# Gated delta rule on one Trainium2 core: the chunk's decay matrix from running sums that are loaded from DRAM, in place of a matrix product

## The chip, the cores and the metric

The kernel runs on one core of one Trainium2 chip, in one launch. The metric is the device time in microseconds. Three runs of the kernel before gave 3124.35, 3131.32 and 3132.2 us, with a median of 3131.32 us.

## The reference

Two layers are computed on x of shape (2, 1024, 256). The first adds a gated delta rule and a routed feed-forward part to x, the second a small chunked linear attention and a sparse feed-forward part. The change touches the first layer's delta rule and the gates that feed it:

```python
beta = jax.nn.sigmoid(b)
g = -jnp.exp(A_log) * jax.nn.softplus(a + dt_bias)
...
def step(S, inp):
    qt, kt, vt, gt, bt = inp
    S = S * jnp.exp(gt)[:, None, None]
    kv = jnp.einsum('hk,hkv->hv', kt, S)
    delta = (vt - kv) * bt[:, None]
    S = S + kt[:, :, None] * delta[:, None, :]
    o = jnp.einsum('hk,hkv->hv', qt, S)
    return (S, o)
```

There are 2 batches, 16 key heads and 32 value heads of width 128, and g is never positive. A chunk of 128 tokens is computed at once. For that each unit (one batch and one value head) needs the matrix exp(G_n - G_p) for tokens n >= p and zero elsewhere, where G is the running sum of g within the chunk. It weighs both the matrix that is solved for the deltas and the one that gives the outputs.

## The kernel before, in words

`front` normalizes and turns the input, `routed_loop` does the routed feed-forward part and, at its end, the gates (`gate_sums` and what follows), `delta_rule` does the delta rule, and `second_layer` the second layer. Only `delta_rule` and the gates in `routed_loop` are touched.

`delta_rule` takes 128 steps, one for each of the 16 key heads (outer) and 8 chunks (inner), and each step holds U = 4 units, 2 batches by 2 value heads. The steps are pipelined by hand over slots: in slot s each engine runs its own `body(s)`, a fixed list of pieces, and each piece works on the step that lies a fixed number of slots back. `S_P = 0` is the projection and the convolution's four taps, `S_S = 1` the SiLU, `S_F = 2` norms, decay matrix, key-query product (`causal` on PE) and scaled values, `S_L = 5` the triangular solve's blocks of 64, `S_D = 6` the state's step, and `S_E = 7` the output projection. Every engine goes through its list in order, and what it waits for is a semaphore in the piece. A loop body holds 16 slots; 16 slots ahead of it and the last 11 behind it are written out.

What PE does in a slot, with the line numbers of the profile: `front_tp` (L622), `state_in` (L522, the state times keys and queries), `x64` (L598), `x16` (L539), `decay` (L633, the running sums' differences as one 128 x 128 by 128 x 512 product), `causal` (L645), `w1` (L555), `w64` (L609), `project(0)` (L680), `solve` (L709), `w2` (L568), `values` (L659), `apply` (L720, L723), `project(1)` (L680), `w3` (L581, L584), `gated_tp` (L734), `zproj` (L697), `project_out` (L749).

The decay matrix goes through four engines. POOL makes `gtri` = mask times g (L377, in `step_gates`), PE multiplies it by a mask (L633), ACT takes the exponential into `ET` (`expo`, L862), and POOL zeroes its lower half (`causal` on POOL, L406). DVE uses `ET` in `strict` (writes `N`, L1121) and `attention` (L1134).

ACT's last pieces in a slot are `evac(1)` (copies `raw` and `conv` out of the second projection's bank, L907 and L908), `squares` (four squares of the gated output with a sum, L895) and `gtev` (copies the turned output into `gT`, L927). `project_out` on PE starts with

```python
                    pe.wait_ge(gT_rdy, t.done())
```

The base blocks of the solve are found on POOL by substitution (`base_first`, `base_rest`) for two steps at a time. `N` goes to DRAM and comes back as `Bk` in another layout, and the results go out and come back as `Tp` and `Wp`. SP issues these transfers and the heads' weights (`weights`), all on one queue and in program order.

## Time and profile before

| | |
|---|---|
| median of three runs | 3131.32 us |
| the profiled execution's own time | 3119.58 us |
| its span, first to last instruction | 3117.6 us |
| mean granted TensorE clock | 0.979 |
| PE busy | 2977.7 us, 96% of the span |
| DVE, ACT, POOL busy | 2341.5, 1771.9, 1693.4 us (75, 57, 54%) |
| steps of `delta_rule` | 128, from 306.8 us (first projection) to about 2786 us (last output projection) |

A timeline row gives the start in us from the span's start, the duration in us, the engine, the line, the operation, what it writes and reads, and in brackets the idle time of the engine ahead of it with what ended it. One row can stand for several instructions (x8). A product in 32-bit floats is recorded as two matmuls. PE is matmul, PEld the weight load ahead of it.

### The profile page before, as it was taken

To read this page: it belongs to the slowest core of one execution; us is meant where nothing else is said; L and a number is where in the kernel's file an instruction comes from. 1 tells how busy PE (TensorE), PEld (TensorE's weight loads), DVE (VectorE), ACT (ScalarE), POOL (GpSimd) and SP (SyncE) were. 2 spreads that over 40 slices of the span, in tenths; PEclk is the share of its full clock that TensorE was granted. 3 is DMA by queue.
4 is the path that set the end of the run, shared out by engine and by line. 5 is a ranking of instruction groups with operands and counts; after the bars stand their busy time and mean duration, and the time that the engine had idled before them with its cause. 6 is when DMAs were issued, how large, how long until landed. Compare 5 with 4: busy or idle time off the path is not lost. (4 is left out here: it accounts for less than half of the span.)

```text
span 3117.6 us, 70222 instructions
## 1 busy us (share of the span) xinstructions
PE 2977.7 (96%) x23017; PEld 2174.3 (70%) x23017; DVE 2341.5 (75%) x4933; ACT 1771.9 (57%) x5794; POOL 1693.4 (54%) x3744
## 2 busy tenths in 40 slices
PE   5998699999999999999999999999999999978998
PEld 4556377777777777777777777777777777764655
DVE  3433588888888888888888888888888888746766
ACT  4322466666666666666666666666666666532332
POOL 2000466676666766676767666766766767610000
PEclk9999799999999999999999999999999999978999
DMA  3000111112112111111111212121111111210000
GB/s 85 1 1 14 27 44 37 44 37 45 42 44 46 40 44 42 44 37 45 37 44 37 47 42 50 39 48 38 44 37 44 37 44 37 46 38 4 7 7 14
DMA packets 447088, 113.77 MB, mean 36 GB/s; under 512 B 350528, under 2 KB 445872, under 8 KB 446704
## 3 DMA queue, kind: packets, MB, share of 16 engines
q1 hardware_dynamic: 446704, 108.99, 15.7%
q8 instruction: 200, 3.28, 0.4%
q14 instruction: 184, 1.51, 0.2%
HBM read 63.85 MB, written 45.09 MB: 35 GB/s over the span
## 5 line engine op out<-in xcount | busy, mean ns | idle before, releaser
L907 ACT ACTIVATE raw<-bank 128x512 f32<-128x512 f32 x256 | 153.3, 599 | 428.8 <-PE bank L680 423.4
L464 POOL TENSOR_TENSOR Tb<-Tb,btmp 64x14 f32<-64x14 f32 (+6 forms) x896 | 327.5, 365 | 70.9 <-POOL btmp L460 1.2
L1175 DVE SCALAR_TENSOR_TENSOR conv<-raw,ckq,conv 128x512 f32<-128x512 f32 x384 | 323.7, 843 | 24.2 <-ACT conv L908 13.2
L460 POOL TENSOR_TENSOR btmp<-Bk,Tb 64x14 f32<-64x14 f32 (+6 forms) x896 | 296.6, 331 | 65.6
L1175 DVE SCALAR_TENSOR_TENSOR conv<-raw,cv,conv 128x512 f32<-128x512 f32 x384 | 292.1, 761 | 13.8 <-ACT conv L908 2.7
L680 PE MATMUL bank<-xnT,wkq 128*128 128x512 f32 x512 | 254.8, 621 | 17.4 <-issue 11.8
L448 POOL TENSOR_SCALAR Tb<-Bk 64x256 f32<-64x256 f32 x64 | 73.7, 1151 | 341.2 <-DMA Bk<-blk_n 341.2
L680 PE MATMUL bank<-xnT,wv 128*128 128x512 f32 x512 | 248.8, 609 | 7.0 <-issue 4.7
L749 PE MATMUL bank<-wout_h,gT 128*128 128x256 f32 x1024 | 249.6, 387 | 1.3 <-ACT gT L927 1.2
L522 PE MATMUL bank<-S,ykq 128*128 128x256 f32 x1024 | 243.2, 379 | 5.8 <-issue 5.8
L852 ACT ACTIVATE sq_kq<-bank 128x128 bf16<-128x128 f32 x512 | 134.9, 278 | 194.6 <-PE bank L622 194.6
L1145 DVE SCALAR_TENSOR_TENSOR S<-S,gs,bank 128x128 f32<-128x128 f32 x512 | 143.7, 343 | 132.4 <-PE bank L720 132.4
L697 PE MATMUL bank<-wz_h,xnT 128*128 128x256 f32 x1024 | 242.4, 380 | 0.0
L406 POOL TENSOR_TENSOR ET<-ET,le 128x512 f32<-128x512 f32 x128 | 179.8, 1405 | 90.9 <-ACT ET L862 90.9
L749 PEld LDWEIGHTS bank<-wout_h,gT 128*128 128x128 f32 x1024 | 186.1, 192 | 43.3 <-ACT gT L927 22.7
L884 ACT ACTIVATE vb<-bank,ty 128x128 f32<-128x128 f32 x512 | 146.5, 369 | 114.2 <-PE bank L659 114.2
L522 PEld LDWEIGHTS bank<-S,ykq 128*128 128x128 f32 x1024 | 184.6, 190 | 26.7 <-issue 7.0
L697 PEld LDWEIGHTS bank<-wz_h,xnT 128*128 128x128 f32 x1024 | 184.6, 190 | 19.9
L709 PEld LDWEIGHTS bank<-R,Wf 128*128 128x128 f32 x1024 | 136.5, 195 | 62.6 <-issue 62.6
L1121 DVE SCALAR_TENSOR_TENSOR N<-ET,ty,bank 128x128 f32<-128x128 f32 x512 | 143.4, 341 | 44.5 <-POOL ET L406 37.6
L895 ACT ACTIVATE sq_gat<-gat 128x128 bf16<-128x128 f32 x512 | 150.7, 304 | 33.1 <-DVE gat L1160 33.1
L939 ACT ACTIVATE gatn<-gat,ty 128x128 f32<-128x128 f32 x512 | 161.9, 390 | 0.1
(350 smaller groups left out, 7543.3 us busy)
## 6 DMA issues: line engine op xcount, KB each, us to landing
blk_n<-N SPq DMA_DIRECT2D x128, 256.0 KB, 2.6
Tp<-blk_t SPq DMA_DIRECT2D x128, 128.0 KB, 2.9
Wp<-blk_w SPq DMA_DIRECT2D x128, 128.0 KB, 3.0
wkq<-in_L_attn_W_qkvz_dram SPq DMA_DIRECT2D x32, 128.0 KB, 2.4
wv<-in_L_attn_W_qkvz_dram SPq DMA_DIRECT2D x16, 256.0 KB, 3.1
Bk<-blk_n SPq DMA_DIRECT2D x64, 64.0 KB, 2.7
blk_t<-Tb SPq DMA_DIRECT2D x64, 64.0 KB, 2.5
blk_w<-Wb SPq DMA_DIRECT2D x64, 64.0 KB, 2.5
```

What stands on the lines that cost most here:

```text
L406: pool.tensor_tensor(ET[:], ET[:], le4[:], ALU.mult).then_inc(ET_rdy, 1)
L460: pool.tensor_tensor(tmp, Bk[:, j, j + 1:].unsqueeze(2).broadcast_to([64, 15 - j, j]), Tb[:, j, 0:j].unsqueeze(1).broadcast_to([64, 15 - j ...
L464: pool.tensor_tensor(Tb[:, j + 1:, 0:j], Tb[:, j + 1:, 0:j], tmp, ALU.subtract).then_inc(row_rdy, 1)
L522: i = pe.matmul(bB[6 + j][:, b], chunk(kq_of(t), t, j, b), S[:, 2 * b:2 * b + 2, :].rearrange("p v n -> p (v n)"), start=True, stop=True)
L680: i = pe.matmul(bank[1 - j][:], w[:, k, j * P:(j + 1) * P], xnT[:, k, q * 512:(q + 1) * 512].rearrange("p (c b n) -> p b c n", c=2, b=B), ...
L697: i = pe.matmul(bB[1][:, b], xnT[:, k, n * P:(n + 1) * P], wz[:, k, :], start=(k == 0), stop=(k == KT - 1))
L749: i = pe.matmul(bB[0][:, h], gT[:, 2 * h + v, :], wout[:, v, :], start=(v == 0), stop=(v == 1))
L884: i = act.activation(vb[t.c % RING][:, u, :], bU[0][:, u], ACT.Copy, scale=ty[t.c][:, VS, u // 2:u // 2 + 1])
L895: i = act.activation(junkg[:, u, :], gat[:, u, :], ACT.Square, accum_out=ty[t.c][:, SSG, u:u + 1])
L907: act.activation(raw[h][:, j, :, 3:], bB[1 - j], ACT.Copy)
L939: i = act.activation(gatn[:, u, :], gat[:, u, :], ACT.Copy, scale=ty[t.c][:, SC, u:u + 1])
L1175: dve.scalar_tensor_tensor(out=conv[h][:, j], in0=raw[h][:, j, :, k:k + 256], scalar=cw[:, j, k:k + 1], in1=conv[h][:, j], op0=ALU.mult, o ...
```

## The change

`gate_sums` already makes the running sums of g within each chunk. `routed_loop` now also copies them (`ab`), keeps them with the other per-token gates (kind `CUM` in the place of `G`), turns them with four transposes, and writes them to DRAM as `decay_rows`, with one row of 128 sums per chunk and unit.

In `delta_rule`, SP loads for each step the four rows onto all 128 partitions (`decays`, 256 KB into one of two tiles `rowb`), a slot before they are used. ACT makes Relu(G_p - row) in place (`clamp`, four instructions, one for each unit) and then exp(-x) into `ET` (`expo`). Both now stand at the end of the slot before the one that uses `ET`. The product on PE, its operand on POOL, and their semaphores are gone. POOL's list is in another order, the copy of the level-64 block into `Wf` goes from DVE (`add_w64`) to ACT (`wev64`), and DVE's six taps of the convolution stand together, alternating between their two halves, with `add_w3` ahead of them.

```diff
-G, BETA, NGAM, GAM, DEC, GLAST = range(NKIND)
+CUM, BETA, NGAM, GAM, DEC, GLAST = range(NKIND)
...
+                def decays(s):
+
+                    t = s.back(S_F - 2)
+                    if not t.live:
+                        return
+                    free = held(sp, t.done(2))
+                    sp.wait_ge(m["made"], 2)
+                    sp.wait_ge(hd["rows_out"], 16)
+                    wait(sp, exp_rdy, free)
+                    sp.dma_start(rowb[t.c % 2][:].rearrange("p (b v) n -> p b (v n)", b=B),
+                                 rows[t.c, :, bass.ds(t.head(), 1), :].rearrange("b h n -> b (h n)").partition_broadcast(P)
+                                 ).then_inc(rowb_in[t.c % 2], 16)
...
                 def body(s):
+                    decays(s)
                     weights(s)
                     base_out(s)
                     dump(s)
...
-                    pool.wait_ge(gs_rdy, t.done())
-                    wait(pool, dt_mm, t.done(1))
-                    pool.tensor_tensor(gtri[:], le4[:], gs[t.c][:, G, :].unsqueeze(2).broadcast_to([P, U, P]),
-                                       ALU.mult).then_inc(gtri_rdy, 1)
...
                 def body(s):
+                    step_gates(s)
+                    causal(s)
                     derive(s)
-                    causal(s)
                     halo(s)
                     base_rest(s)
-                    step_gates(s)
                     base_first(s)
...
-                def decay(s):
-
-                    t = s.back(S_F)
-                    if not t.live:
-                        return
-                    pe.wait_ge(gtri_rdy, t.done())
-                    wait(pe, zz_rdy, t.done(4))
-                    ends(pe, s, araw_rdy, t, -1)
-                    pe.matmul(bank[1][:], m["gt"][:], gtri[:].rearrange("p u n -> p (u n)"), start=True,
-                              stop=True).then_inc(dt_mm, 1)
...
-                        wait(pe, exp_rdy, t.done(2))
+                        wait(pe, zz_rdy, min(t.done(6), STEPS) if t.i is None else t.done(6))
...
+
+                def clamp(s):
+
+                    t = s.back(S_F - 1)
+                    if not t.live:
+                        return
+                    act.wait_ge(rowb_in[t.c % 2], t.pairs(16, 16))
+                    act.wait_ge(gs_rdy, t.done())
+                    for u in range(U):
+                        i = act.activation(rowb[t.c % 2][:, u, :], rowb[t.c % 2][:, u, :], ACT.Relu, scale=-1.0,
+                                           bias=gs[t.c][:, CUM, u:u + 1])
+                    i.then_inc(rel_rdy, 1)
+
                 def expo(s):
-                    t = s.back(S_F)
-                    if not t.live:
-                        return
-                    act.wait_ge(dt_mm, t.done())
+
+                    t = s.back(S_F - 1)
+                    if not t.live:
+                        return
+                    act.wait_ge(rel_rdy, t.done())
                     wait(act, N_rdy, t.done(1))
                     wait(act, attn_rdy, t.done(1))
-                    act.activation(ET[:], bU[1], ACT.Exp).then_inc(exp_rdy, 1)
+                    act.activation(ET[:], rowb[t.c % 2][:], ACT.Exp, scale=-1.0).then_inc(exp_rdy, 1)
 
                 def kdec(s):
...
 
+                def wev64(s):
+
+                    t = s.back(S_L + 1)
+                    if not t.live:
+                        return
+                    act.wait_ge(w64_mm, t.done())
+                    act.activation(Wf[0:64, :, 64:], bG[5][0:64], ACT.Copy).then_inc(w64_rdy, 1)
...
                     xev64(s)
-                    expo(s)
                     normed(s)
+                    wev64(s)
                     evac(s, 0)
                     vscale(s)
                     kdec(s)
                     evac(s, 1)
+                    clamp(s)
                     squares(s)
                     gtev(s)
+                    expo(s)
...
                     dve.tensor_tensor(gat[:].rearrange("p u n -> p (u n)"), gat[:].rearrange("p u n -> p (u n)"),
                                       zz[:].rearrange("p b n -> p (b n)"), ALU.mult).then_inc(gat_rdy, 1)
 
-                def taps(s, j):
+                def taps(s):
 
                     t = s.back(S_P)
                     if not t.live:
                         return
                     h = t.c % 2
                     cw = cv if h else ckq
-                    done = tap_b if j else tap_a
-                    dve.wait_ge(braw_rdy if j else araw_rdy, t.done())
+                    dve.wait_ge(araw_rdy, t.done())
+                    dve.wait_ge(braw_rdy, t.done())
                     for k in (2, 1, 0):
-                        if k < 2:
-                            dve.wait_ge(done[k + 1], t.done())
-                        dve.scalar_tensor_tensor(out=conv[h][:, j], in0=raw[h][:, j, :, k:k + 256],
-                                                 scalar=cw[:, j, k:k + 1], in1=conv[h][:, j], op0=ALU.mult,
-                                                 op1=ALU.add).then_inc(done[k], 1)
+                        for j, done in enumerate((tap_a, tap_b)):
+                            if k < 2:
+                                dve.wait_ge(done[k + 1], t.done())
+                            dve.scalar_tensor_tensor(out=conv[h][:, j], in0=raw[h][:, j, :, k:k + 256],
+                                                     scalar=cw[:, j, k:k + 1], in1=conv[h][:, j], op0=ALU.mult,
+                                                     op1=ALU.add).then_inc(done[k], 1)
...
-                    taps(s, 0)
                     add_w3(s)
-                    taps(s, 1)
+                    taps(s)
                     norm_apply(s)
...
+                def gate_rows():
+
+                    pe.wait_ge(act_rdy, 5)
+                    for q in range(4):
+                        i = pe.transpose(psB[:, 0, q * P:(q + 1) * P], ab[:, q * P:(q + 1) * P], m["ident"][:])
+                    i.then_inc(cum_rdy, 1)
...
                 for j, kind in enumerate((GAM, DEC, GLAST)):
                     for b in range(B):
                         i = act.activation(into(kind, b), of(psH[:, j, :], b), ACT.Exp)
                 i.then_inc(act_rdy, 1)
+
+                act.wait_ge(cum_rdy, 2)
+                act.activation(turned, psB[:, 0, :], ACT.Copy).then_inc(turned_rdy, 1)
+
+            @block.sync
+            def _(sp):
+                sp.wait_ge(turned_rdy, 1)
+                sp.dma_start(rows.rearrange("(q c) b h (v n) -> (c b h v) q n", q=4, v=2),
+                             turned.rearrange("p (q n) -> p q n", q=4)).then_inc(hd["rows_out"], 16)
 
             @block.vector
             def _(v):
...
-                        v.tensor_copy(into(G, b), of(ga[:], b))
                         v.tensor_copy(into(BETA, b), of(gf, b))
 
                 def gate_end():
 
                     v.wait_ge(act_rdy, 5)
+                    for b in range(B):
+                        v.tensor_copy(into(CUM, b), of(ab[:], b))
+                    v.wait_ge(act_rdy, 6)
```

Three places in program order. First ACT in a steady slot, from the second projection's copies to the next slot's squares of keys and queries (`sq_kq`). Before:

```order
L907 ACTIVATE raw<-bank 128x2x256
L908 ACTIVATE conv<-bank,ckq 128x512
L895 ACTIVATE sq_gat,ty<-gat 128x128 x4
L927 ACTIVATE gT<-bank,nw 128x2x2x64 x2
L832 ACTIVATE zz<-bank 128x512
L852 ACTIVATE sq_kq,ty<-bank 128x128 x4
```

The same stretch of ACT in the changed program:

```order
L920 ACTIVATE raw<-bank 128x2x256
L921 ACTIVATE conv<-bank,ckq 128x512
L863 ACTIVATE rowb<-rowb,gs 128x128 x4
L908 ACTIVATE sq_gat,ty<-gat 128x128 x4
L948 ACTIVATE gT<-bank,nw 128x2x2x64 x2
L875 ACTIVATE ET<-rowb 128x512
L830 ACTIVATE zz<-bank 128x512
L850 ACTIVATE sq_kq,ty<-bank 128x128 x4
```

Four instructions on `rowb` now stand between `conv` and `sq_gat`, and the exponential stands between `gT` and `zz`; it stood behind `Xs` before.

Second PE in a steady slot, from the gated output's transposes to the first projection. Before:

```order
L734 MATMUL bank<-ident,gatn 128x128 x4
L697 MATMUL bank<-wz_h,xnT 128x256 x4
L749 MATMUL bank<-wout_h,gT 128x256 x4
L622 MATMUL bank<-ident,ykq 128x128 x4
L522 MATMUL bank<-S,ykq 128x256 x4
L598 MATMUL bank<-Tp,N 64x64 x4
L539 MATMUL bank<-Tp,N 64x64 x8
L633 MATMUL bank<-gtri,gt 128x512
L645 MATMUL bank<-ykq 128x256 x2
L555 MATMUL bank<-Wp,Xs 64x64 x8
L609 MATMUL bank<-Wf,Xs 64x64 x4
L680 MATMUL bank<-xnT,wv 128x512 x2
```

The same stretch of PE in the changed program, from the output projection on:

```order
L748 MATMUL bank<-wout_h,gT 128x256 x4
L633 MATMUL bank<-ident,ykq 128x128 x4
L533 MATMUL bank<-S,ykq 128x256 x4
L609 MATMUL bank<-Tp,N 64x64 x4
L550 MATMUL bank<-Tp,N 64x64 x8
L645 MATMUL bank<-ykq 128x256 x2
L566 MATMUL bank<-Wp,Xs 64x64 x8
L620 MATMUL bank<-Wf,Xs 64x64 x4
L680 MATMUL bank<-xnT,wkq 128x512 x2
```

The product with `gtri` is gone; the rest stands as it stood.

Third SP's queue where a head's value weights `wv` are loaded, once in eight slots. Before:

```order
L315 DMA Tp<-blk_t 64x8x64 x2
L320 DMA Wp<-blk_w 64x8x64 x2
L332 DMA blk_n<-N 128x4x128
L281 DMA wv<-in_L_attn_W_qkvz_dram 128x2x256
L282 DMA cv<-in_L_attn_conv_w_dram 128x2x4
```

The same place in the changed program:

```order
L329 DMA Tp<-blk_t 64x8x64 x2
L334 DMA Wp<-blk_w 64x8x64 x2
L346 DMA blk_n<-N 128x4x128
L304 DMA rowb<-decay_rows 128x2x256
L282 DMA wv<-in_L_attn_W_qkvz_dram 128x2x256
L283 DMA cv<-in_L_attn_conv_w_dram 128x2x4
```

The row load stands ahead of the weights in the queue.

## Rows read from the trace of the kernel before

**Rows 1.** Table by stretch: start:end, length, busy us by engine, clock, DMA

```profile
1500.00:2000.00 500.00, 498.83 (x4343) 377.24 (x4342) 417.40 (x888) 330.03 (x1124) 344.93 (x758) 1.00 0.19 41
```

**Rows 2.** Timeline of PE over one slot

```profile
1543.58 1.06 PE L720 MATMUL bank<-Us,kd 128*128 128x128 f32 x8
...
1545.37 1.88 PE L680 MATMUL bank<-xnT,wv 128*128 128x512 f32 x4
1547.18 0.62 PE L581 MATMUL bank<-Xs,Wk 64*64 64x64 f32 x7
...
1550.48 1.92 PE L749 MATMUL bank<-wout_h,gT 128*128 128x256 f32 x8
...
1555.39 1.13 PE L633 MATMUL bank<-gtri,gt 128*128 128x512 f32 x2
1556.36 1.03 PE L645 MATMUL bank<-ykq 128*128 128x256 f32 x4
1557.31 0.51 PE L555 MATMUL bank<-Wp,Xs 64*64 64x64 f32 x10
...
1560.03 1.05 PE L709 MATMUL bank<-R,Wf 128*128 128x128 f32 x8
...
1562.12 1.06 PE L720 MATMUL bank<-Us,kd 128*128 128x128 f32 x8
```

**Rows 3.** Timeline of ACT in the same slot

```profile
1547.29 0.60 ACT L907 ACTIVATE raw<-bank 128x512 f32<-128x512 f32 x1 [1.33 <-PE bank L680]
1547.78 0.68 ACT L908 ACTIVATE conv<-bank,cv 128x512 f32<-128x512 f32 x1
1548.35 0.31 ACT L895 ACTIVATE sq_gat<-gat 128x128 bf16<-128x128 f32 x1
...
1549.52 0.83 ACT L927 ACTIVATE gT<-bank,nw 128x256 f32<-128x256 f32 x2
1550.68 0.60 ACT L832 ACTIVATE zz<-bank 128x512 f32<-128x512 f32 x1 [0.33 <-PE bank L697]
...
1556.56 0.60 ACT L862 ACTIVATE ET<-bank 128x512 f32<-128x512 f32 x1 [0.16 <-PE bank L633]
1557.05 1.26 ACT L939 ACTIVATE gatn<-gat,ty 128x128 f32<-128x128 f32 x4
1560.23 0.60 ACT L907 ACTIVATE raw<-bank 128x512 f32<-128x512 f32 x1 [1.92 <-PE bank L680]
```

**Rows 4.** Waits of the whole span: who for whom, total us, times, longest

```profile
PEld bank L749 <- ACT gT L927: 22.7, 126, 0.8
```

**Rows 5.** Timeline of PE's weight loads in the same slot

```profile
1550.40 1.59 PEld L749 LDWEIGHTS bank<-wout_h,gT 128*128 128x128 f32 x8 [0.17 <-ACT gT L927]
```

**Rows 6.** Groups of instructions by line: busy us, mean ns, idle before

```profile
L939 ACT ACTIVATE gatn<-gat,ty 128x128 f32<-128x128 f32 x512 | 161.9, 390 | 0.1
```

**Rows 7.** Timeline of DVE in the same slot

```profile
1544.68 1.12 DVE L1145 SCALAR_TENSOR_TENSOR S<-S,gs,bank 128x128 f32<-128x128 f32 x4 [1.05 <-PE bank L720]
...
1547.71 2.32 DVE L1175 SCALAR_TENSOR_TENSOR conv<-raw,cv,conv 128x512 f32<-128x512 f32 x3
...
1555.81 0.41 DVE L1057 TENSOR_TENSOR Xs<-bank,mkP 128x256 f32<-128x256 f32 x1
...
1558.32 0.42 DVE L992 COPY Wf<-bank 64x256 f32<-64x256 f32 x1 [0.97 <-PE bank L609]
```

**Rows 8.** Waits from 1000 to 2400 us

```profile
PE bank L680 <- DMA cv<-in_L_attn_conv_w_dram: 2.3, 3, 1.0
PE bank L539 <- DMA Tp<-blk_t: 1.9, 4, 1.0
```

**Rows 9.** DMA issues: number, size, median us from issue to landing

```profile
blk_n<-N SPq DMA_DIRECT2D x128, 256.0 KB, 2.6
```

**Rows 10.** Timelines of ACT and DVE at the end of `routed_loop`

```profile
300.08 2.09 ACT L1736 ACTIVATE gates<-psH 128x256 f32<-128x256 f32 x6 [18.27 <-PE psH L1632]
...
302.61 0.17 DVE L1829 MEMSET gates<- 128x128 f32 x1
```

More of the change, by code:

```diff
@@ L106, in masks, with delta_rule @@
     return m
-def delta_rule(nc, ins, m, l2, hd, acc, xn, xnT, gates):
+def delta_rule(nc, ins, m, l2, hd, acc, xn, xnT, gates, rows):
     S_P, S_S, S_F, S_L, S_D, S_E = 0, 1, 2, 5, 6, 7
@@ L132, in delta_rule @@
         le4 = sb("le4", [P, U, P])
-        gtri = sb("gtri", [P, U, P])
+        rowb = [sb(f"rowb{r}", [P, U, P]) for r in range(2)]
         ET = sb("ET", [P, U, P])
@@ L199, in delta_rule @@
         tap_b = {k: ev(f"tap{k}b_rdy") for k in (2, 1, 0)}
-        (gs_rdy, gtri_rdy, ET_rdy, halo_rdy, sse_rdy, nrm_rdy, nn_rdy, der_rdy, o1_rdy, o2_rdy, o3_rdy, sc_rdy) = (
-            ev(n) for n in ("gs_rdy", "gtri_rdy", "ET_rdy", "halo_rdy", "sse_rdy", "nrm_rdy", "nn_rdy", "der_rdy",
+        (gs_rdy, ET_rdy, halo_rdy, sse_rdy, nrm_rdy, nn_rdy, der_rdy, o1_rdy, o2_rdy, o3_rdy, sc_rdy) = (
+            ev(n) for n in ("gs_rdy", "ET_rdy", "halo_rdy", "sse_rdy", "nrm_rdy", "nn_rdy", "der_rdy",
                             "o1_rdy", "o2_rdy", "o3_rdy", "sc_rdy"))
+        rowb_in, rel_rdy = [ev(f"rowb{r}_in") for r in range(2)], ev("rel_rdy")
         base_in, tmp_rdy, row_rdy, base_rdy = ev("base_in"), ev("tmp_rdy"), ev("row_rdy"), ev("base_rdy")
@@ L691, in zproj @@
                     wait(pe, araw_rdy, min(t.done(-S_L), STEPS) if t.i is None else t.done(-S_L))
-                    ends(pe, s, exp_rdy, t, S_F - S_L)
                     ends(pe, s, zz_rdy, t, 1)
@@ L984, in _ @@
                 dve.wait_ge(setup, 5)
-                def add_w64(s):
-                    t = s.back(S_D)
-                    if not t.live:
-                        return
-                    dve.wait_ge(w64_mm, t.done())
-                    dve.tensor_copy(Wf[0:64, :, 64:], bG[5][0:64]).then_inc(w64_rdy, 1)
                 def accumulate(s):
@@ L1571, in _, with routed_loop @@
                 v.wait_ge(r_rd, 1)
-def routed_loop(nc, ins, m, r, x, xn, xnT, gates):
+def routed_loop(nc, ins, m, r, hd, x, xn, xnT, gates, rows):
     w1T, w2A, b1c, b2r, b1a, b1d, b2m, topw, wsum, sel, z1T, rb, wba, dtb, alog, xnS = (r[k] for k in (
@@ L1589, in routed_loop @@
         ga = sb("g_all", [P, NT * HV])
[L1590 removed]
+        ba_rdy, act_rdy, dve_rdy, cum_rdy, turned_rdy, gate_self = (
+            sem("g_" + n) for n in ("ba", "act", "dve", "cum", "turned", "self"))
+        turned = xn[:, 0:2, :].rearrange("p n d -> p (n d)")
         steps = gates[:].rearrange("p (kh c) k u -> p kh c k u", c=C)
@@ L1733, in _ @@
                 act.wait_ge(cum_rdy, 1)
+                act.activation(ab[:], psH[:, 0, :], ACT.Copy).then_inc(act_rdy, 1)
                 for j, kind in enumerate((GAM, DEC, GLAST)):
@@ L2333, in build @@
             gates = c2.enter_context(nc.sbuf_tensor("gates", [P, STEPS, NKIND, U], F32))
+            rows = nc.dram_tensor("decay_rows", (C, B, HK, 2 * P), F32, kind="Internal").ap()
             hd = {k: c2.enter_context(nc.sbuf_tensor(k, sh, F32)) for k, sh in (
@@ L2339, in build @@
                 front(nc, ins, m, l2, r, hd, x, xn, xnT)
-                routed_loop(nc, ins, m, r, x, xn, xnT, gates)
-            delta_rule(nc, ins, m, l2, hd, x, xn, xnT, gates)
+                routed_loop(nc, ins, m, r, hd, x, xn, xnT, gates, rows)
+            delta_rule(nc, ins, m, l2, hd, x, xn, xnT, gates, rows)
         second_layer(nc, ins, m, l2, x, xn, xnT, out)
```

11 lines of the change are left out of this document (5 added, 6 removed).

## The prediction, on record before the changed kernel ran

> **What bounds the kernel now.** I read the table by stretch first. In the 500 us from 1500 on, PE is busy for 498.83, at the full granted clock, while ACT has work for 330 and DVE for 417 [rows 1]. So inside `delta_rule` the time of a slot is the sum of what PE does in it. PE's timeline over one slot then gives the lengths, as differences of starts: `apply` begins at 1543.58 and the next one at 1562.12, so a slot is 18.54 us, and no idle time is named in between [rows 2]. 128 slots of 18.54 us are 2373 us of the 3117.6 us span. What PE no longer does in a slot is gained 128 times, as long as no other engine is late for it.
>
> Who is nearly late? The list of waits names one pair that occurs in 126 of the 128 slots: the weight load of the output projection waits for `gT` from ACT, 22.7 us in all [rows 4]. In the slot shown the weight load waits for 0.17 us and starts at 1550.40, and the matmuls start at 1550.48 [rows 5, 2]. PE itself loses nothing, but ACT hands over `gT` at the last moment. ACT's timeline shows what stands ahead of it [rows 3]: ACT is idle for 1.33 us until the second projection is done (1547.18, where the next product starts on PE [rows 2]), and from 1547.29 it works without a gap through `raw`, `conv`, four squares and `gT` until 1550.35. That is a chain from PE to ACT and back to PE: 3.30 us from 1547.18 to 1550.48, and PE has exactly 3.30 us of other work in it (`w3`, the transposes, the z projection). ACT's idle time lies elsewhere in the slot, where it waits for PE.
>
> **The change part by part.**
>
> *The product leaves PE.* From its start at 1555.39 to the next start at 1556.36 it takes 0.97 us [rows 2]. If nothing else moved, 128 x 0.97 = 124.2 us would be gained.
>
> *The four Relus join ACT's chain.* They stand between `conv` and the squares, hence after the second projection and before `gT`: the stretch in which ACT has no slack. Their price is from start to start of four 128x128 instructions that read SBUF with one operand per partition. The squares have this shape: four of them, each with its read-out, take 1.17 us from 1548.35 to 1549.52. `gatn`, with a scale per partition, takes 1.26 us for four with the last one's tail, so (1.26 - 0.39)/3 = 0.29 each, and 1.16 for four [rows 3, 6]. I take 1.17 us. Bounds: no less than one instruction of the same 512 columns, `conv`, 0.57 us from start to start, and no more than four without overlap, 4 x 0.39 = 1.56 [rows 3, 6]. The value lies at `gatn`, which it is nearest to. Nothing hides it: PE would start `project_out` 1.17 us later, less the slack that is left. The weight load led the matmuls by 0.08 us [rows 5, 2], so I give 0.03 us of slack. The waits for the load of the rows and for the gates should cost nothing, since the load is issued a slot earlier and the nearest transfer, `N`'s dump of the same 256 KB, lands in 2.6 us [rows 9]. 128 x (1.17 - 0.03) = +145.9 us.
>
> The Trainium skill, "ScalarE: Activation LUTs", section "Rules for kernel authors", says that relu belongs on VectorE and not on ScalarE. Here DVE has four 128x128 instructions in 1.12 us [rows 7], so the engine's speed makes no difference; the place does. By that rule the sum would lose the +145.9 and keep most of the -124.2, as DVE waits 1.05 us for PE in each slot.
>
> *The exponential moves behind `gT`.* It delays `zz`'s tanh: `gT` ends at 1550.35 and the tanh started at 1550.68 [rows 3], and 0.5 us of exponential in that 0.33 us gap makes it late by about 0.2 us. DVE needs the tanh only after the taps, some 3 us later. On the old place it leaves 0.5 us of room. Cost 0; without the cover, 0.2 us a slot.
>
> *The level-64 copy goes from DVE to ACT.* It took 0.42 us on DVE after a wait of 0.97 for PE [rows 7], from 1558.32 on. ACT stands behind `gatn` then, with 1.92 us of idle time ahead of its next work (1560.23), and `solve` needs the copy at 1560.03 [rows 3, 2]. Cost 0 with about 1.3 us of cover, and no gain on DVE, which waits for PE there anyway.
>
> *The taps alternate.* Three in a chain take 2.32 us [rows 7], 0.77 each; without the chain I estimate 0.6, so up to 1 us less on DVE, of which part goes to waiting for `w3` and for both halves of `conv`. DVE's stretch from `S` (1544.68) to the end of `Xs` (1556.22) has no gap, and PE takes up `Xs` only at 1557.31, 1.09 us later [rows 7, 2]. With the later `project_out` this slack grows by another 0.2 us. Gain 0 in my forecast.
>
> *POOL* loses `gtri`, and its masking no longer waits within the slot. POOL is ahead of PE in the steady slots. Where it is late, transfers are late too: PE waited 1.9 us for `Tp` and 2.3 us for `cv` in 1400 us [rows 8], some 7 us over the 128 slots. I give back 3 us of it.
>
> *The row loads* are queued ahead of the weights on SP. At a head's second chunk `wv` and `cv` go out one issue later, about 0.6 us; that wait is in the 7 us above, and the deadline is later now too. Cost 0, with the bound below.
>
> *The end of `routed_loop`.* ACT makes a copy of 0.6 us ahead of its exponentials, which ended at 302.17, and another one behind them, DVE's last work ended at 302.78 [rows 10], and the barrier waits for SP's issue: +1.2 us.
>
> Sum: -124.2 + 145.9 - 3 + 1.2 = +19.9 us. A slot becomes 18.54 - 0.97 + 1.14 = 18.71 us. Against its own profiled execution (3119.6 us, span 3117.6) the kernel after takes 3139.5. The three runs shown have a median of 3131.3, 0.4% above that execution, so I add the 20 us to the median: **3151 us**.
>
> **The rivals.**
>
> 1. *ACT hides the Relus* (the other side: faster). ACT has work for two thirds of a slot only, so the Relus could cost nothing, and PE would gain the whole 0.97. This holds if PE doesn't in truth need `gT` by 1550.48, that is if more than 1 us of slack is hidden behind the modelled ends of the matmuls. From 0.97 us of slack on it decides. Then DVE's chain comes within 0.12 us (1.09 - 0.97) of binding, and the alternating taps would earn something. 3131 - 124 + 1 = 3008 us. For it speaks only the 57% of ACT; against it the 126 waits for `gT`. Chance 0.12.
>
> 2. *Gain and loss cancel.* With 1.0 us for the four Relus, or 0.15 us of slack at `gT`, a slot ends within 0.05 us of 18.54. The rest, 1.2 - 3 us and up to 7 us given back by transfers that are on time, makes 3122 to 3138. For it: both terms are near 1 us, and their difference is a sixth of either. Chance 0.17.
>
> 3. *The row loads are in the way.* Each puts 256 KB more on the one queue. If all of the 2.6 us of such a transfer [rows 9] came on top at the head's second chunk, where PE already waited for `cv`, it would cost 16 x 2.6 = 42 us more, or the same if a clamp in eight waits for its rows: up to 3193. Against it: on most slots SP has nothing to issue for ten microseconds. Chance 0.09.
>
> 4. The forecast, ACT's chain as worked out: chance 0.62, of itself 3138 to 3172 (Relus of 1.1 to 1.3 us, 0 to 0.1 of slack).
>
> **How the numbers follow.** The predicted time is case 4's. The range of 3115 to 3180 holds cases 2 and 4 almost whole and the near part of case 3, and leaves out case 1 and most of 3: about 8 in 10. 0.3% is 9.4 us, about what a measurement of this kernel can tell from no change. Faster by more: case 1 and a little of 2, 0.14. Within: most of 2 and the lower end of 4, 0.21. Slower by more: the rest of 4, and 3, 0.65.
>
> **What the profile after would show.** Right: PE is idle for about 1.1 us a slot, all of it ahead of the output projection, with ACT `gT` as releaser; from `apply` to `apply` about 18.7 us; on ACT four instructions on `rowb` in 1.17 us behind `conv`, with no wait ahead of them; DVE waits about 1 us longer in a slot than before. PE busy falls from 2977.7 to about 2854 us. Wrong: if PE shows no idle time there (case 1, slots of 17.6 us); if `gT` waits for something else than the Relus, such as the rows' DMA (case 3); if the Relus take 0.25 us or less each, or if the squares would have waited for DVE's `gat` in any case, since then part of the Relus is hidden.

## The result and the profile after

The changed kernel takes 3174.85 us (median of 4 runs, 3167.3 to 3182.26), the kernel before on the same chip 3131.76 us (4 runs, 3124.35 to 3137.64): a ratio of 1.0139, 95% interval 1.0106 to 1.0172. It is 43 us slower; 20 us slower, 3151 us, was predicted. The profiled execution took 3182.26 us (span 3180.4, mean granted clock 0.974); against the profiled one of before that is 62.8 us of span and not 43, since this execution is the slowest of the four and the profiled one of before (3119.58 us) was faster than all four runs of before. The changed kernel's own profile is therefore used for where the time goes, and the medians for how much it is.

The page after gives the busy time of each engine, share of the span and instructions:

```profile
PE 2911.2 (92%) x22765; PEld 2132.7 (67%) x22765; DVE 2258.0 (71%) x4805; ACT 1956.3 (62%) x6436; POOL 1520.6 (48%) x3616
```

PE lost 66.5 us of work and the span grew by 62.8: PE now waits. The list of waits of PE from 400 to 2700 us says for whom (who for whom and at which line, total us, times, longest):

```profile
PE bank L748 <- ACT gT L948: 109.9, 119, 0.9
PE bank L680 <- DMA cv<-in_L_attn_conv_w_dram: 16.1, 10, 3.0
PE bank L680 <- DMA ckq<-in_L_attn_conv_w_dram: 3.5, 9, 0.7
PE bank L566 <- ACT Xs L930: 1.9, 1, 1.9
```

Before, the first pair had its wait in the weight load alone [rows 4] and PE had 2.3 us for `cv` in a shorter stretch [rows 8]. One slot on PE, from the z projection to the next output projection and on:

```profile
1518.95 1.89 PE L696 MATMUL bank<-wz_h,xnT 128*128 128x256 f32 x8
1521.76 1.99 PE L748 MATMUL bank<-wout_h,gT 128*128 128x256 f32 x8 [0.92 <-ACT gT L948]
...
1563.26 1.99 PE L748 MATMUL bank<-wout_h,gT 128*128 128x256 f32 x8 [0.92 <-ACT gT L948]
1565.09 0.60 PE L633 MATMUL bank<-ident,ykq 128*128 128x128 f32 x4
...
1568.25 1.13 PE L645 MATMUL bank<-ykq 128*128 128x256 f32 x4
1569.40 0.56 PE L566 MATMUL bank<-Wp,Xs 64*64 64x64 f32 x12
...
1582.21 1.13 PE L748 MATMUL bank<-wout_h,gT 128*128 128x256 f32 x4 [0.92 <-ACT gT L948]
```

An undisturbed slot is 1582.21 - 1563.26 = 18.95 us here and 18.93 in most of the trace, where it was 18.54 [rows 2]. ACT's rows of the same place, from the second projection's copies on:

```profile
1517.49 0.60 ACT L920 ACTIVATE raw<-bank 128x512 f32<-128x512 f32 x1 [1.33 <-PE bank L680]
1517.98 0.68 ACT L921 ACTIVATE conv<-bank,ckq 128x512 f32<-128x512 f32 x1
1518.56 1.27 ACT L863 ACTIVATE rowb<-rowb,gs 128x128 f32<-128x128 f32 x4
1519.72 0.30 ACT L908 ACTIVATE sq_gat<-gat 128x128 bf16<-128x128 f32 x1
...
1520.89 0.82 ACT L948 ACTIVATE gT<-bank,nw 128x256 f32<-128x256 f32 x2
1521.61 0.62 ACT L875 ACTIVATE ET<-rowb 128x512 f32<-128x512 f32 x1
```

It is the chain of [rows 3] with four Relus in it: 1518.56 to 1519.72 is 1.16 us, no wait stands ahead of them, `gT` ends at 1521.71 and PE starts 0.05 us later.

In eight of the 16 heads the slot in which the head's `cv` is first needed is much longer, 20.3 to 24.8 us; the one shown is 22.57 us, from 1521.76 to 1544.33. PE in that slot, and below it what SP issued (the second number is the time of the issue, not of the transfer):

```profile
1528.42 0.45 PE L620 MATMUL bank<-Wf,Xs 64*64 64x64 f32 x5
1530.75 3.68 PE L680 MATMUL bank<-xnT,wv 128*128 128x512 f32 x4 [1.87 <-DMA cv<-in_L_attn_conv_w_dram]
```

```profile
1523.36 0.56 SPq L346 DMA_DIRECT2D blk_n<-N  x1
1524.18 0.39 SPq L304 DMA_DIRECT2D rowb<-decay_rows  x1
1524.80 0.37 SPq L282 DMA_DIRECT2D wv<-in_L_attn_W_qkvz_dram  x1
1525.39 0.37 SPq L283 DMA_DIRECT2D cv<-in_L_attn_conv_w_dram  x1
```

`cv` is 4 KB; it is issued at 1525.39 behind 256 KB of rows and 256 KB of weights, and PE gets it at 1530.7. Then the projection takes 3.68 us instead of the 1.98 that the same line takes in the next slots (at 1551.37 and 1570.32). The table by stretch (start:end, length, busy us of PE, PEld, DVE, ACT, POOL, granted clock, DMA share, GB/s) shows the clock:

```profile
1515.00:1528.00 13.00, 12.06 (x98) 8.97 (x98) 11.66 (x25) 10.11 (x38) 9.12 (x21) 1.00 0.41 88
1530.75:1534.26 3.51, 3.51 (x4) 1.48 (x5) 0.00 (x0) 0.00 (x0) 0.00 (x0) 0.51 0.30 79
1534.30:1540.00 5.70, 5.70 (x50) 4.28 (x48) 3.56 (x9) 3.35 (x10) 3.86 (x11) 1.00 0.10 11
```

Behind the idle 1.87 us the granted clock is 0.51, the lower of PE's two levels (1.2 GHz), and at 1534.30 it is 2.4 GHz again. So this late `cv` is paid twice. Not every one is: behind waits of 1.29 us (at 2454.54) and 1.41 us (at 2607.48) the projection takes its 1.98.

### The profile page after: what moved, and what is told of

Its sections match the earlier page's. It is cut to its first block and busy times, and to the rows that moved or that the text cites. A ratio compares the mean times of both kernels' runs of the same rounds, so it can differ in the third digit from the quotient of the medians.

```text
span 3180.4 us, 70682 instructions
## 1 busy us (share of the span) xinstructions
PE 2911.2 (92%) x22765; PEld 2132.7 (67%) x22765; DVE 2258.0 (71%) x4805; ACT 1956.3 (62%) x6436; POOL 1520.6 (48%) x3616
## 3 DMA queue, kind: packets, MB, share of 16 engines
q1 hardware_dynamic: 482048, 142.81, 20.7%
## 5 line engine op out<-in xcount | busy, mean ns | idle before, releaser
L748 PE MATMUL bank<-wout_h,gT 128*128 128x256 f32 x1024 | 258.4, 396 | 114.2 <-ACT gT L948 114.2
L475 POOL TENSOR_TENSOR Tb<-Tb,btmp 64x14 f32<-64x14 f32 (+6 forms) x896 | 281.4, 314 | 70.1
L471 POOL TENSOR_TENSOR btmp<-Bk,Tb 64x14 f32<-64x14 f32 (+6 forms) x896 | 253.7, 283 | 65.6
L680 PE MATMUL bank<-xnT,wv 128*128 128x512 f32 x512 | 259.5, 631 | 23.7 <-DMA cv<-in_L_attn_conv_w_dram 16.1
L1191 DVE SCALAR_TENSOR_TENSOR conv<-raw,ckq,conv 128x512 f32<-128x512 f32 x384 | 262.1, 751 | 20.7 <-ACT conv L921 18.7
L1191 DVE SCALAR_TENSOR_TENSOR conv<-raw,cv,conv 128x512 f32<-128x512 f32 x384 | 265.5, 757 | 7.4 <-ACT conv L921 5.4
L1122 DVE TENSOR_TENSOR Us<-bank,ty 128x512 f32<-128x512 f32 x128 | 88.5, 692 | 218.2 <-PE bank L708 218.2
L442 POOL TENSOR_TENSOR ty<-ty 128x4 f32<-128x4 f32 x128 | 47.5, 371 | 313.7 <-ACT sq_gat L908 313.7
L448 POOL TENSOR_TENSOR ty<-ty,mhalf 128x4 f32<-128x4 f32 x128 | 174.5, 1363 | 10.7
L417 POOL TENSOR_TENSOR ET<-ET,le 128x512 f32<-128x512 f32 x128 | 163.4, 1277 | 29.4 <-ACT ET L875 29.4
```

The costliest lines, as they stand in the source:

```text
L417: pool.tensor_tensor(ET[:], ET[:], le4[:], ALU.mult).then_inc(ET_rdy, 1)
L448: pool.tensor_tensor(y[:, O1, :], y[:, O2, :], mhalf[:], ALU.pow).then_inc(o3_rdy, 1)
L471: pool.tensor_tensor(tmp, Bk[:, j, j + 1:].unsqueeze(2).broadcast_to([64, 15 - j, j]), Tb[:, j, 0:j].unsqueeze(1).broadcast_to([64, 15 - j ...
L475: pool.tensor_tensor(Tb[:, j + 1:, 0:j], Tb[:, j + 1:, 0:j], tmp, ALU.subtract).then_inc(row_rdy, 1)
L680: i = pe.matmul(bank[1 - j][:], w[:, k, j * P:(j + 1) * P], xnT[:, k, q * 512:(q + 1) * 512].rearrange("p (c b n) -> p b c n", c=2, b=B), ...
L748: i = pe.matmul(bB[0][:, h], gT[:, 2 * h + v, :], wout[:, v, :], start=(v == 0), stop=(v == 1))
```

## Experiments

All ratios are to the kernel before, run on the same chip, with their 95% interval. Its medians were 3121.5 us (13 runs) beside the first four kernels, 3122.1 (10) beside the next four and 3118.0 (11) beside the last three; beside `after`, which below means the changed kernel, it was 3131.8. So `after` is compared with an experiment by the difference of their ratios, not of their medians. A "clean slot" is one in which nothing is late: the length that most slots of a trace have, from one start of the output projection to the next. Each trace has 120 slots of full length; the last seven, in which the pipeline empties, are shorter.

**1. The Relus out of the stretch ahead of `gT`.** In `after`'s list on ACT:

```diff
                     kdec(s)
+                    clamp(s)
                     evac(s, 1)
-                    clamp(s)
                     squares(s)
```

> The changed kernel, with the four Relus moved ahead of the copies of the second projection on ACT, into the 1.33 us in which ACT waits for that projection. The theory (the Relus cost time because they stand between the second projection and gT): PE no longer waits ahead of the output projection, a slot falls from 18.94 us to about 17.8 us, and the time to 3045 us (3030 to 3075). A rival, that the row loads or the longer ACT list as such cost the time, has it at 3160 to 3175 us, as nothing but the place of four instructions changes.

Measured: 3125.1 us (10 runs), ratio 1.0015 (1.0001 to 1.0028). The mechanism held: PE's waits for `gT` fell to 0.3 us. A clean slot is 17.82 us, about the 17.8 expected. The time is not: 3045 was expected, and 80 us more were measured. PE's waits from 400 to 2700 us show what came up:

```profile
PE bank L680 <- DMA cv<-in_L_attn_conv_w_dram: 45.7, 15, 3.6
PE bank L719 <- DVE Us L1122: 20.8, 42, 1.3
PE bank L566 <- issue: 5.4, 31, 0.2
```

With shorter slots the wait for `cv` is nearly three times as long as in `after` and comes in every head: 15 slots, eight apart, are 20.7 to 24.0 us long. DVE's `Us` is next. Followed up in 5.

**2. The Relus alone, in the kernel before.** Four Relus of the same form on a tile `fill`, whose result nobody reads, between `conv` and the squares; the product stays:

```diff
+                    for u in range(U):
+                        act.activation(fill[:, u, :], fill[:, u, :], ACT.Relu, scale=-1.0,
+                                       bias=gs[t.c][:, GAM, u:u + 1])
...
                     evac(s, 1)
+                    four(s)
                     squares(s)
```

> The kernel before, with four 128x128 Relus on a tile of their own put between conv and the squares on ACT, and nothing else changed. The theory: PE is held up by 1.16 us less 0.07 us of slack in every slot, 128 x 1.09 = 140 us, so 3271 us (3255 to 3290). The rival, that ACT with work for 57% of the span hides four short instructions: 3131 us.

Measured: 3245.18 us (4 runs), ratio 1.0398 (1.0377 to 1.0419), 124 us more, below the 3255 to 3290 expected. PE waited for `gT` 106.8 us in 116 slots, 0.92 each; the rest is the weight load, as below. The rival, that the Relus hide, is excluded. The clean slot is 1528.11 - 1508.41 = 19.70 us, 1.16 more than the 18.54 of before: here four Relus cost PE what they take, although ACT has work for 57% of the time only. That 120 such slots don't make 139 us has another cause. Before, the 120 full slots are 2246.6 us long (from 424.7 to 2671.3), 22 more than 120 x 18.54: in 28 of them something is more than 0.1 us late. With the Relus they are 2370.5 us long, only 7 more than 120 x 19.70. The longer slot has swallowed 15 us of lateness.

**3. The product alone taken out of the kernel before.** The exponential reads `gtri` in SBUF instead of the product's bank, so that `ET` doesn't hold the decays:

```diff
-                    decay(s)
...
-                    act.activation(ET[:], bU[1], ACT.Exp).then_inc(exp_rdy, 1)
+                    act.activation(ET[:], gtri[:], ACT.Exp).then_inc(exp_rdy, 1)
```

> The kernel before without the decay product on PE: the exponential reads the product's operand gtri in SBUF instead, so ET does not hold the decays. Nothing else moves. By the row of before the product is worth 0.97 us a slot, 124 us: 3007 us. By the trace of the changed kernel, where the key-query product without the decay product ahead of it takes 0.2 us longer to the next start, it is worth 0.77 us: 99 us, so 3033 us. If DVE's or POOL's chain binds before that: 3040 to 3060 us, with waits on PE for Xs or Us.

Measured: 3079.27 us, ratio 0.9865 (0.9847 to 0.9883): 42 us gained, a third of 128 x 0.97 = 124, and near the 3040 to 3060 expected if DVE or POOL binds. Two causes stand in the trace. A slot without a named wait (`apply` at 1502.04 and at 1519.92) is 17.88 us, not 17.57, and one reason is a pair of rows in it, `causal`'s product and `w1`:

```profile
1513.85 1.13 PE L645 MATMUL bank<-ykq 128*128 128x256 f32 x4
1515.11 0.51 PE L555 MATMUL bank<-Wp,Xs 64*64 64x64 f32 x10
```

They stand 1.26 us apart, where it was 0.95 [rows 2]. In the slot before it (output projection at 1491.16), 17.77 us long, they are 1.15 apart (1496.08 and 1497.23). The other 0.11 is by the trace a wait for `Xs`: DVE ends it at 1514.85, 0.26 us ahead of `w1` at 1515.11, where in the kernel before it was 1.09 ahead. So the product on PE also covered the way from `x16` over DVE to `w1`. And PE's waits from 400 to 2700 us, with DVE for the most part, make other slots longer than that:

```profile
PE bank L719 <- DVE Us L1105: 29.1, 41, 1.5
PE bank L555 <- DVE Xs L1055: 8.5, 12, 1.4
PE bank L680 <- DMA cv<-in_L_attn_conv_w_dram: 8.4, 13, 1.2
PE bank L539 <- DMA Tp<-blk_t: 8.3, 9, 2.8
```

**4. The weights ahead of the row load**, in `after`'s list on SP:

```diff
                 def body(s):
-                    decays(s)
                     weights(s)
+                    decays(s)
                     base_out(s)
```

> The changed kernel, with the row load behind the weight loads in SP's list instead of ahead of them. If the row loads make the weights late (16 us of waits for cv and 3.5 us for ckq on PE, and some half-speed clock behind the longest), the time falls by 12 to 20 us, to 3155 to 3163 us. If those waits come from the weights being issued late anyway, it stays within 5 us of 3175.

Measured: 3148.95 us (4 runs), ratio 1.0087 (1.0069 to 1.0105). By the ratios that is 16 us less than `after`, give or take 12, as the theory had it; by the medians, measured beside different runs of the kernel before, 26. PE waits for `cv` 0.6 us in all, `cv` lands 3.1 us after its issue instead of 5.1, and all but four of the full slots are clean (1509.20, 1528.12, 1547.03: 18.92 each). The transfers are the same as in `after` and only their order differs, so it is the order that makes `cv` late. The output projection's rows, with their first and last start, sum up `delta_rule`: before, `after`, and weights first:

```profile
L749 PE MATMUL bank<-wout_h,gT x1024: 379/379/796, 424.7 to 2784.5; 128*128 128x256 f32 x171
```

```profile
L748 PE MATMUL bank<-wout_h,gT x1024: 379/379/793, 428.9 to 2842.5; 128*128 128x256 f32 x171
```

```profile
L748 PE MATMUL bank<-wout_h,gT x1024: 379/379/793, 429.6 to 2811.5; 128*128 128x256 f32 x171
```

From first to last that is 2359.8, 2413.6 and 2381.9 us: between these two traces the row loads ahead of the weights cost 31.7 us. The trace of `after` is of its slowest run, 7.3 us above its median. So the place of the row loads is worth 16 to 32 us, by how it is read.

**5. Both edits**, Relus early and weights first.

> The changed kernel with both edits: the four Relus between kdec and the second projection's copies on ACT, and SP issues the weights ahead of the row load. Theory: with the Relus out of the stretch between the second projection and the output projection, what is left of the loss is PE's wait for cv behind the row load (45.7 us between 400 and 2700 us with the Relus early) and the lower clock behind it. Without them I expect 3070 to 3095 us on a chip where the kernel before takes 3121, that is a ratio of 0.983 to 0.992. Rival: the slot is now bound by DVE and POOL (N waits for POOL's masking), the waits move there and the time stays within 10 us of the 3125 of the Relus early alone.

Measured: 3076.14 us (4 runs), ratio 0.9853 (0.9834 to 0.9872), as the theory had it. By the ratios the two faults of `after` together are worth 89 us, and the change without them is a gain; against 1, the weights first are worth 51 us. A clean slot is 17.82 us, and about half of the slots are over 0.1 us longer. Slots of 17.83, 18.59, 17.82, 19.39 and 18.40 us follow each other (1503.71, 1521.54, 1540.13, 1557.95, 1577.34, 1595.74): PE's waits are 24.7 us for `Us`, 47 times, and 7.8 for `cv`. DVE's rows of the slot of 19.39 us show where `Us` is held up:

```profile
1564.87 0.41 DVE L1081 TENSOR_TENSOR Wk<-Wp,bank 128x256 f32<-128x256 f32 x1
1568.56 1.12 DVE L1136 SCALAR_TENSOR_TENSOR N<-ET,ty,bank 128x128 f32<-128x128 f32 x4 [3.29 <-POOL ty L408]
1569.60 0.68 DVE L1122 TENSOR_TENSOR Us<-bank,ty 128x512 f32<-128x512 f32 x1
```

DVE stands at `N` for a small result of POOL, and `Us` stands behind `N`. POOL had no gap to speak of: base rows until 1562.3, `ET`'s mask from 1565.11, and that result at 1568.19.

**6. The taps and the level-64 copy alone, in the kernel before.** The diff is that of the change, `taps` and `wev64`.

> The kernel before with only two pieces of the change: DVE's six taps alternate behind add_w3, and the level-64 copy goes from DVE to ACT. Theory (the prediction's steps that cost nothing): PE binds, both pieces lie in idle time, no change: ratio 0.998 to 1.002. Rival: the taps of the first half now wait for the second half's conv and for w3, and ACT's copy pushes what stands behind it, so PE waits for Xs or Us: up to 0.2 us a slot, 25 us slower, ratio 1.008. The other side: DVE is relieved and PE's few waits for DVE go, at most 5 us.

Measured: 3108.82 us (5 runs), ratio 0.9959 (0.9944 to 0.9975): 13 us gained where I and the theory had nothing, and more than the "at most 5 us" of the other side.

**7. The Relu on DVE**, ahead of the state's update, with the weights first:

```diff
+                    for u in range(U):
+                        i = dve.tensor_scalar(rowb[t.c % 2][:, u, :], rowb[t.c % 2][:, u, :], gs[t.c][:, CUM, u:u + 1],
+                                              0.0, ALU.subtract, ALU.min)
...
                     add_w2(s)
+                    clamp(s)
                     update(s)
```

> The changed kernel with the Relu as subtract and min on DVE, four 128x128 instructions ahead of the state's update, where DVE waited for PE for about 1 us in the kernel before, and with the weights ahead of the row load on SP. Theory: ACT's stretch between the second projection and the output projection is as short as before, so PE no longer waits for gT, and the new work on DVE costs at most its excess over the idle 1.05 us: ratio to the kernel before 0.978 to 0.990. Rival: DVE's chain through the update, gat and attention is late by those 1.1 us and the squares on ACT wait for gat, so that PE waits for gT all the same: 3145 to 3165, ratio near 1.01.

Measured: 3077.14 us (4 runs), ratio 0.9857 (0.9835 to 0.9878). It is the same as in 5, 72 us less than in 4. DVE did the four in the time in which it had waited for PE ahead of `S`:

```profile
1559.97 0.86 DVE L1173 TENSOR_SCALAR rowb<-rowb,gs 128x128 f32<-128x128 f32 x4
1561.10 1.12 DVE L1147 SCALAR_TENSOR_TENSOR S<-S,gs,bank 128x128 f32<-128x128 f32 x4 [0.27 <-PE bank L719]
```

**8. The row loads alone.** The kernel before, with 256 KB (two rows of W_out on all partitions) loaded in each step into tiles that nobody reads, ahead of the weights:

```diff
+                    wait(sp, exp_rdy, free)
+                    wait(sp, rowb_in[t.c % 2], last)
+                    sp.dma_start(rowb[t.c % 2][:].rearrange("p (b v) n -> p b (v n)", b=B),
+                                 ins["L0_attn_W_out"][bass.ds(t.head(2), 2), :].partition_broadcast(P)
+                                 ).then_inc(rowb_in[t.c % 2], 16)
...
+                    decays(s)
                     weights(s)
```

> The kernel before with one addition: for each step SP loads 256 KB, two rows of W_out on all 128 partitions, into one of two tiles that nothing reads, at the place in SP's list where the changed kernel has its row load, ahead of the weights. It tells what the transfers alone cost. Theory: PE waits for cv once in eight steps for 1 to 3 us more and runs at the lower granted clock for a while behind the longer waits: 15 to 35 us, ratio 1.005 to 1.011, and cv lands about 5 us after its issue. Rival: the transfers are hidden as I predicted, and in the changed kernel cv was late for another reason: ratio within 1.002.

Measured: 3138.55 us (6 runs), ratio 1.0055 (1.0035 to 1.0075), 16.5 us: transfers that I costed at nothing cost this much by themselves. PE waited 11.6 us for `Tp` (15 times, up to 2.4) and 6.9 for `cv`. The sum is as the theory had it; that most of the waiting is for `Tp` is not, and `cv` landed 3.9 us after its issue, not about 5. The stand-in is lighter than the real load: both bring 256 KB a step, but it adds 18 thousand packets to the run and the rows of `after` 35 thousand, and it lands in 4.0 us where they take 5.2. How far `Tp` late is due to the place in the queue or to the load on the transfer engines was not tried apart.

**9. The taps alone, in the kernel before**, with the copy left on DVE.

> The kernel before with one piece of the change: DVE's six taps alternate behind add_w3; the level-64 copy stays on DVE. With both pieces the kernel was 0.41% faster than before (0.9944 to 0.9975), though I had costed both at nothing. Theory: the taps are what gives that, since DVE has less work ahead of the next slot's blocks and PE's few waits for DVE and for Tp (which comes late when N is late) go: ratio 0.994 to 0.998. Rival: it is the copy, which stands in DVE's list ahead of N and Us and waits there for PE: then the taps alone give 0.999 to 1.001.

Measured: 3105.25 us (6 runs), ratio 0.9959 (0.9943 to 0.9974), the whole gain of 6. The copy is worth nothing that the runs can tell. The clean slot is 18.54 us as before, but 18 of the 120 full slots are over 0.1 us longer, where it was 28, even in the slowest of the six runs, which the trace is of.

**10. The function table loaded early.** In the kernel of 5, an exponential of one column behind the logarithm:

```diff
                 act.activation(l1[:], l1[:], ACT.Ln, bias=1.0).then_inc(act_rdy, 1)
+                act.activation(scrap[:], alog[:, 0:1], ACT.Exp)
                 act.wait_ge(cum_rdy, 1)
```

> The kernel with the Relus early and the weights first, and one instruction more: a one-column exponential of a scrap value right behind the logarithm in the gates, ahead of the wait for the running sums, so that ACT's function table for the exponential is loaded while ACT waits. Expected in the trace: no table load between the copy of the running sums and the exponentials, the end of the gates 1.3 us earlier or a little more (the first projection at about 308 to 309 us, against 310.5), and a time 1 to 4 us below that of the same kernel without it, less than the measurement can tell. Rival: the load was hidden behind the copy's neighbours anyway and the first projection stays at 310.

ACT's rows at the gates, in `after` and in this kernel:

```profile
301.77 0.60 ACT L1758 ACTIVATE ab<-psH 128x512 f32<-128x512 f32 x1 [19.57 <-PE psH L1648]
302.38 1.28 ACT L1761 ACT_TABLE_LOAD   x1
303.68 2.09 ACT L1761 ACTIVATE gates<-psH 128x256 f32<-128x256 f32 x6
```

```profile
301.87 0.60 ACT L1760 ACTIVATE ab<-psH 128x512 f32<-128x512 f32 x1 [18.05 <-PE psH L1649]
302.36 2.09 ACT L1763 ACTIVATE gates<-psH 128x256 f32<-128x256 f32 x6
```

The load of 1.28 us is out of the chain. The copy `gth` on ACT, where the gates begin, starts at times that differ by 2 us between runs; from there to the first projection it is 33.1 us (276.12 to 309.21) against 34.5 in `after` (276.01 to 310.53) and in 5 (275.31 to 309.82): 1.4 us gained. 3072.98 us (5 runs), ratio 0.9846 (0.983 to 0.9862), not to be told from 5 by the time.

**11. `Us` ahead of `N`**, in the kernel of 10:

```diff
-                    strict(s)
                     uscale(s)
+                    strict(s)
```

> The kernel with the early exponential table, and on DVE the scaling of the deltas (Us, for which PE waits) ahead of N in the slot's list. In the kernel with Relus early and weights first PE waited 24.7 us for Us in 47 slots, where DVE had stood at N, waiting up to 3.3 us for a small result of POOL. Theory: those waits go, and the lower clock behind them; N is late by up to 1 us more, which has slots of room: ratio to the kernel before 0.974 to 0.981. Rival: N's dump and the base blocks behind it become late, PE waits for Tp or Wp instead, and the ratio stays at 0.984 to 0.987.

Measured: 3178.82 us (5 runs), ratio 1.0188 (1.0173 to 1.0204): 106 us slower than 10, so theory and rival are both wrong in size, the rival right in kind. PE no longer waits for `Us`, but, from 400 to 2700 us:

```profile
PE bank L550 <- DMA Tp<-blk_t: 43.0, 59, 2.0
PE bank L566 <- DVE Xs L1072: 26.6, 60, 0.6
PE bank L680 <- DMA cv<-in_L_attn_conv_w_dram: 24.8, 15, 3.2
```

`N` used to be made while DVE waited for `Us`'s product. Now DVE idles there (2.66 us in one slot) and makes `N` afterwards, in the stretch from `Us` to the next slot's `Xs`, which has no gap; so `Xs` is late in every second slot, and `N`'s way over DRAM to `Tp` starts late in all. These waits sum to 94 us where they were 11 us in 10, and 26.5 us for `Us` are gone, so by the lists some 60 us of the 106 are new waits. PE's busy time is 47 us longer too (2936.3 against 2888.9) for the same instructions; the lower clock behind the waits would do that, but it was not taken apart.

## Why the prediction was right in its direction and half in its size

*What bounds.* Right: PE's slot, with `gT` just in time. Experiments 1, 2 and 5 show it from three sides.

*The four Relus join ACT's chain.* Right to a few hundredths: 1.16 us on ACT against 1.17, and the output projection starts 2.81 us behind the z projection (1518.95 to 1521.76), where it was 1.73; the start of the z projection in the kernel before is this row, the other stands in [rows 2]:

```profile
1548.75 1.89 PE L697 MATMUL bank<-wz_h,xnT 128*128 128x256 f32 x8
```

The output projection is 0.07 us longer too (1.99 against 1.92); its weight load, which had led by 0.08 us, now waits for `gT` as well. That is 1.15 a slot against my 1.14, and experiment 2, which has the Relus alone, lengthens the clean slot by 1.16.

*The product leaves PE.* This is the first term that was mis-sized. I took its 0.97 us from start to start. But `causal`'s product to `w1` is now 1569.40 - 1568.25 = 1.15 us, where it was 0.95 (1556.36 to 1557.31 [rows 2]); experiment 3 has 1.26. So a slot gains 0.77: 25 us less over 128 slots. Experiment 3 says the same: its clean slots are 17.77 us, 0.77 below 18.54, as long as `w1` needn't wait for `Xs` as well. Half of the missing 0.2 us lies in `causal`'s product itself, 1.13 us where it was 1.03. The weight loads, before and in `after`, show a reason:

```profile
1555.93 0.19 PEld L645 LDWEIGHTS bank<-ykq 128*128 128x128 f32 x1 [0.24 <-issue]
```

```profile
1568.24 0.73 PEld L645 LDWEIGHTS bank<-ykq 128*128 128x128 f32 x4
```

Before, `causal`'s first load ran beside the removed product, 0.43 us ahead of its own matmul; in `after` all four start with the product. That this is the cause was argued and not tried, and the other 0.1 us, between `causal`'s end and `w1`, stays open. With 0.77 and 1.15 the slot becomes 18.92, and it is 18.92 to 18.95.

*Late transfers given back.* I gave 3 us, from the named waits for DMA. This term was mis-sized too. The 120 full slots before are 22 us longer than 120 clean ones (experiment 2); with the weights first they are 2271.7 us, 1 us longer than 120 x 18.92. So some 20 us of lateness are gone. Experiment 2, which keeps the old taps, gives back 15 of them by longer slots alone; how the rest divides between the taps and the slots was not taken apart.

*The taps, gain 0.* Wrong in the kernel before, where they gained 13 us; in `after` their share may be less, by the term above. The 1.09 us of slack at `Xs` in the one slot that I read is not what every slot has: in the next slot DVE ends `Xs` at 1575.41 and PE takes it up at 1575.85. PE's waits for `Tp` from 400 to 2700 us fell from 7.2 to 3.7 us. *The level-64 copy, 0*: right as far as the runs can tell.

*The row loads, 0.* Wrong, and with the product the largest miss: 16 us by the ratios of `after` and experiment 4, 32 by their traces. It is my third rival, at 0.4 to 0.75 of its price of 42 us; I gave it 0.09. What failed is the sentence that `cv` goes out one issue, 0.6 us, later. The issue is only that much later, but the landing is 2 us later (3.1 us after the issue with the weights first, 5.1 behind the rows), and PE's next projection runs at the lower clock, which costs 1.7 us where the wait itself was 1.87. The Trainium skill, "DMA: Bandwidth & Descriptors", section "Queues, rings and completion order", gives a reason why 4 KB wait for 512: on each transfer engine the write that signals a completion lands only after all earlier writes of that engine. The trace agrees so far: by the medians `wv` lands 4.9 us after its issue and `cv`, issued 0.59 us later, 5.1 after its own, so the small transfer lands just behind the large one. Whether the signal or the bytes are held up no run here tells.

*The end of `routed_loop`, 1.2.* The first projection is 3.75 us later (310.53 against 306.78), but 1.69 of that is there before the change does anything (`gth` at 276.01 against 274.32; it moves by 2 us between runs). From `gth` to the first projection it is 34.52 us, where it was 32.46: +2.06. The copies are there as I said; I missed that a copy ahead of the exponentials takes the table load out of ACT's idle time (it stood at 280.53 before) and puts it behind the wait. Experiment 10 takes back 1.4.

Sum between the two profiled spans: clean slots 0.39 x 120 = +47, lateness gone -20, row loads +31, the first output projection 4 us later, the last seven slots 4 us shorter, and 5 us behind the last output projection (337.9 us against 333.1), where nothing was changed: 63, and it is 62.8. The medians differ by 43.

*How much is luck.* The clean slot came out 0.21 us above my 18.71, 25 us in 120 slots, nearly all of it the product. The row loads are 16 to 32 us that I had at nothing, and some 17 us more lateness was given back than I thought. With the lower value that makes 25 + 16 - 17 = 24, and the time is 24 us above my 3151. The errors are of both signs, so that 3175 lies within 3115 to 3180 is in part luck. My sign that PE's work falls to about 2854 us failed: it is 2911.2. 25 of the 57 us are the smaller gain of the product, 9 the output projection's 0.07, some 10 the lower clock behind the six longest waits for `cv` (up to 1.8 each); the rest is open.

*The rivals.* That ACT hides the Relus: excluded by 2. That gain and loss cancel: the two terms are 0.38 apart, not 0.17. On relu's engine: the rule of the Trainium skill in "ScalarE: Activation LUTs", section "Rules for kernel authors", is that relu belongs on VectorE; by the runs that is worth the 72 us of 7 against 4. But 5 has the same gain with the Relus still on ACT, two copies earlier in its list. On this kernel it is the place that counts, as I had it, not the engine. With two lines moved the change is a gain of 1.5%.

## What to carry to other kernels

Work that leaves the bounding engine is worth its start-to-start time only if what it covered has other cover: here 0.77 of 0.97 us, and less where `w1` then waits for `Xs`. Work put on an idle engine costs in full where that engine hands something over just in time (1.16 us a slot), and next to nothing two instructions earlier in its list. For a load added to a queue look at when the small transfers behind it land, not at when they are issued. One slot's timeline is not the mean slot: set the length of all slots against the clean one before counting. An edit to an engine with "slack" gained 13 us here and one of the same kind (11) lost 106.

## What was not expected of the hardware

- A 4 KB transfer landed 5.1 us after its issue behind rows and weights of 256 KB each, and 3.1 us with the row load behind it. In `after` all weights land later too: `wkq` 4.3 us where it was 2.4, `wv` 4.9 where it was 3.1.
- ACT's table load went behind the first instruction that doesn't need it and ahead of the first that does: 1.28 us in the chain, or none, by where one copy stands.
- DVE's subtract and min of four 128x128 tiles took 0.86 us, ACT's four Relus 1.27 us for the same tiles.
- DVE's product `yv` of 128x1024 took 1.21 us at the least and 2.25 in the slot at 1572.70 (experiment 7). POOL had work in the same stretch; what made it longer was not tried.
